# Two chained attention layers on one core: most second-layer blocks take their probabilities from transposed scores, normalised inside the exponential

## What is computed

```
layer 1:  theta, phi, g = W x + b (three 1x1 convolutions)
          y = softmax_m(theta^T phi) g ;  z = (1-w) x + w (Wz y + bz)
layer 2:  q, k (16 channels), v (128) = W z + b
          o = softmax_j(q^T k / 4) applied to v
          result = Wf [gamma*o ; z] + bf
```

## Time and profile before

| | |
|---|---|
| median of 3 runs | 532.09 us (531.92 to 532.65) |
| the profiled execution | 531.95 us, its span 529.9 |
| granted TensorE clock | 1.0 of full speed |
| PE, DVE, ACT, POOL busy | 97%, 76%, 68%, 49% of the span |
| moved by DMA | 15.24 MB, 29 GB/s on average |

### The profile page before, as it was taken

One profiled execution on the slowest core, in us unless ns is written; L12 is line 12 of the kernel. 1 busy time (PEld: TensorE's weight loads), 2 busy tenths in 40 slices (PEclk: granted clock), 3 DMA queues, 4 the chain that ended last, 5 costly groups with the idle time before them and its releaser, 6 DMA issues.

```text
span 529.9 us, 8447 instructions
## 1 busy us (share of the span) xinstructions
PE 516.4 (97%) x2933; PEld 437.1 (82%) x2933; DVE 404.7 (76%) x606; ACT 358.4 (68%) x652; POOL 257.3 (49%) x287
## 2 busy tenths in 40 slices
PE   7998999999999999999999999999999999899996
PEld 5777788888888888888888888888888888788886
DVE  5968676797677877788777887678768786888873
ACT  4865567567785677657776577765777557777763
POOL 1555246575175542864346751558426560354442
PEclk9999999999999999999999999999999999999999
DMA  5100000012000110002000020000200010001001
GB/s 191 45 5 2 7 9 0 2 41 67 9 21 0 67 42 9 21 0 100 17 1 21 1 103 13 1 22 24 83 9 20 2 42 27 9 0 36 13 30 40
DMA packets 6825, 15.24 MB, mean 29 GB/s; under 512 B 1280, under 2 KB 1792, under 8 KB 6784
## 3 DMA queue, kind: packets, MB, share of 16 engines
q1 hardware_dynamic: 6640, 14.57, 8.2%
q10 hardware_dynamic: 144, 0.13, 0.1%
HBM read 8.93 MB, written 4.19 MB: 25 GB/s over the span
## 4 chain that ended last, share of the span: by engine, by line
PE 92%; ACT 3%; DMA 2%; DVE 1%; issue 1%; POOL 0%; SPq 0%; ACTq 0%; DVEq 0%
PE trans L500 20%; PE accum L524 11%; PE accum L526 11%; PE accum L525 11%; PE scores L490 5%; PE scores L466 5%; PE scores L464 5%; PE scores L465 5%; PE misc L551 4%; PE misc L464 3%; PE misc L465 3%; PE misc L466 3%; PE misc L552 1%; DMA x_keep<-x_dram 1%; PE misc L556 1%; ACT probs L636 1%
## 5 line engine op out<-in xcount | busy, mean ns | idle before, releaser
L767 DVE TENSOR_TENSOR pt_lo<-trans,pt_hi 128x512 fp32r<-128x512 f32 x256 | 164.7, 685 | 65.6 <-ACT pt_hi L645 64.4
L645 ACT ACTIVATE pt_hi<-trans 128x512 fp32r<-128x512 f32 x256 | 138.8, 596 | 69.5 <-PE trans L500 67.8
L757 DVE TENSOR_REDUCE neg_max<-scores 128x1 f32<-128x1024 f32 x128 | 155.4, 1214 | 1.1 <-PE scores L466 1.1
L636 ACT ACTIVATE probs<-scores,neg_max 128x1024 f32<-128x1024 f32 x128 | 143.9, 1124 | 4.6 <-DVE neg_max L757 4.6
L500 PE MATMUL trans<-ident,probs 128*128 128x128 f32 x1024 | 133.7, 274 | 2.8 <-ACT probs L636 2.8
L500 PEld LDWEIGHTS trans<-ident,probs 128*128 128x128 f32 x1024 | 115.7, 141 | 14.4 <-ACT probs L636 4.6
L524 PE MATMUL accum<-pt_hi,g_hi 128*128 128x512 f32 x136 | 54.5, 401 | 0.0
L526 PE MATMUL accum<-pt_hi,g_lo 128*128 128x512 f32 x136 | 53.5, 393 | 0.0
L525 PE MATMUL accum<-pt_lo,g_hi 128*128 128x512 f32 x136 | 53.4, 392 | 0.0
L464 PE MATMUL scores<-phi_hi,theta_hi 128*128 128x512 f32 x112 | 48.8, 436 | 0.0
L490 PE MATMUL scores<-k_op,qk_op 128*128 128x512 f32 x128 | 45.4, 435 | 0.0
(11 more groups left out here) (144 smaller groups left out, 947.4 us busy)
## 6 DMA issues: line engine op xcount, KB each, us to landing
x_keep<-x_dram SPq DMA_DIRECT2D x8, 512.0 KB, 3.3
out_dram<-o_sb SPq DMA_DIRECT2D x15, 256.0 KB, 2.4
x_raw<-x_tiles_dram SPq DMA_DIRECT2D x7, 512.0 KB, 3.6
k_op<-qk_op SPq DMA_DIRECT2D x16, 96.0 KB, 2.3
x_raw<-x_tiles_dram SPq DMA_DIRECT2D x2, 256.0 KB, 3.6
...
```

Source lines behind the costliest of these rows:

```text
L636: nc.scalar.activation(probs[:, k % 2, :], scores[:, k % 2, :], ACT.Exp, bias=neg_max[:, k % 4:k % 4 + 1], accum_out=row_sum[:, slot(gb), ...
L645: nc.scalar.activation(pt_hi[:, gb % 2, 4 * bank:4 * bank + 4, t * P:(t + 1) * P], trans[:, cols(bank)].rearrange("p (n q) -> p n q", n=4) ...
L757: nc.vector.tensor_reduce(neg_max[:, k % 4:k % 4 + 1], scores[:, k % 2, :], AX.X, ALU.max, negate=True).then_inc(max_ready, 1)
L767: nc.vector.tensor_tensor(pt_lo[at], trans[:, cols(bank)].rearrange("p (n q) -> p n q", n=4), f(pt_hi[at]), ALU.subtract).then_inc(pt_lo_r ...
```

## The change

Eleven of the sixteen layer-2 blocks (`LATE`: those of index up to 24, the last being set aside as `ASIDE`) are made in another way; the last five, and all of layer 1, keep theirs ("turned").

For a late block PE still makes the scores with queries on the partitions, DVE the maximum, and ACT the exponential, but only for its row sum: the result overwrites the scores. Per pair of units ACT takes the logarithm of the sums; POOL forms `shift` = -max - log(sum) and splits it; SP writes it to a small DRAM tensor `turned` and reads it back along the columns, into two rows of `qk_op` that face ones in `k_op`. Later, nine steps after the block's start, PE multiplies again with the operands exchanged (keys on the partitions, queries along the columns), which gives score minus maximum minus log of the sum, transposed. One exponential of 128x1024 by ACT gives normalised probabilities; POOL rounds them to `pt_hi`, DVE subtracts for `pt_lo`. The value chunks of a late block begin at step 14 after its start instead of 6. No "r" group, diagonals and scaling are left for it: DVE adds the result to the other half and SP stores.

Other edits: `probs` becomes a ring of three tiles `fulls`; `neg_max` has 16 columns; diagonals and `r_rows` lie in tiles that are free by then; g and v of odd images take the tiles `g_hi_0`; the reciprocal waits for the reader of the old one; `k_op` gets two more memsets; ACT loads a function table with exponential and logarithm at the start.

```diff
+LATE = [gb for gb in range(len(BLOCKS)) if BLOCKS[gb][0] == 1 and gb <= 24]
+LATE_STEPS = {gb: tuple(TPB * gb + 9 + j for j in range(CPB)) for gb in LATE}
+LATE_STEPS[24] = (110, 111, 112, 113)
-HURRIED = {0: (6, 6, 7, 7), 1: (10, 10, 11, 11), 30: (126, 126, 127, 127), 31: (128, 128, 130, 131)}
+HURRIED = {0: (6, 6, 7, 7), 1: (10, 10, 11, 11), 24: (114, 114, 115, 115), 27: (116, 116, 117, 117), 30: (126, 126, 127, 127), 31: (128, 128, 130, 131)}
...
+                for gb in LATE:
+                    _, b, h = BLOCKS[gb]
+                    rows = turned[b, h]
+                    for pair in range(2):
+                        if k == TPB * gb + 3 + 2 * pair:
+                            sp.wait_ge(shift_split, 3 * pairs(gb, pair))
+                            sp.dma_start(rows[pair].rearrange("r t p -> p (r t)"), shift_parts[:, h, pair, :, :].rearrange("p r t -> p (r t)"),
+                                         allow_slow_non_contiguous=True).then_inc(shift_out[pair], 16)
+                    if k == TPB * gb + 7:
+                        for pair in range(2):
+                            sp.wait_ge(shift_out[pair], 16 * (LATE.index(gb) + 1))
+                        sp.dma_start(f(qk_op[b % 2][3 * CK:3 * CK + 2, cols(h)]).rearrange("r (q c) -> r q c", q=2),
+                                     rows.rearrange("q r t p -> r q (t p)")).then_inc(shift_in[h], 16)
...
+            def late_scores(gb, j):
+                _, b, h = BLOCKS[gb]
+                pe.wait_ge(shift_in[h], 16 * (b + 1))
+                for bank in range(2):
+                    trans_free(("late", gb, j), bank)
+                    tile = slice((2 * j + bank) * P, (2 * j + bank + 1) * P)
+                    last = nc.tensor.matmul(trans[:, cols(bank)], k_op[b % 2][:, tile], qk_op[b % 2][:, cols(h)],
+                                            start=True, stop=True)
+                last.then_inc(late_scores_ready, 1)
...
+            def pair_log(gb, pair):
+                at = slice(2 * pair, 2 * pair + 2)
+                act.wait_ge(probs_ready, units(TPB * gb + 2 * pair + 1))
...
+                nc.scalar.activation(log_sum[:, BLOCKS[gb][2], at], row_sum[:, slot(gb), at], ACT.Ln).then_inc(log_ready, 1)
...
+            def late_exp(gb, j):
+                act.wait_ge(late_scores_ready, late(gb, j))
+                full_free(act, ("late", gb, j))
+                nc.scalar.activation(full_of(("late", gb, j)), trans[:, :], ACT.Exp).then_inc(late_ready, 1)
...
+            def late_lo(gb, j):
+                dve.wait_ge(late_hi_ready, late(gb, j))
+                pair_free(dve, gb, j)
+                hi, lo = pair_tiles(gb, j)
+                nc.vector.tensor_tensor(lo, full_of(("late", gb, j)), f(hi), ALU.subtract).then_inc(late_lo_ready, 1)
...
+                for gb, j in late_fills(k - 2):
+                    late_lo(gb, j)
+                if 0 <= k - 2 < UNITS and (k - 2) // TPB in TURNED:
+                    unit_lo(k - 2)
...
+            def late_hi(gb, j):
+                pool.wait_ge(late_ready, late(gb, j))
+                pair_free(pool, gb, j)
+                hi, _ = pair_tiles(gb, j)
+                nc.gpsimd.tensor_copy(hi, full_of(("late", gb, j))).then_inc(late_hi_ready, 1)
```

538 lines of the change are left out of this document (325 added, 213 removed).

## The result

The changed kernel takes 534.22 us (median of 9 runs, 534.05 to 537.69) against 532.09 us for the kernel before (9 runs beside it, 531.92 to 534.07): ratio 1.0053, 95% interval 1.0033 to 1.0074. It is 0.5% slower where the forecast was 520.3 us, and it lies outside the range of 511 to 530. The profiled execution took 534.12 us, with a span of 532.3 us.

What follows compares the result with a forecast made beforehand. PE's own instruction stream was taken as the bound (busy 516.4 of 529.9 us). 529.9 - 23.1 + 3.5 + 3.0 + 3.9 + 0 + 1.0 = 518.2 us of span, 520.3 us with 2.05 beyond the span; range 511 to 530.

Steps and rivals of the forecast that it cites:

- What goes from PE: Eleven late blocks: transposes removed, two score matmuls per unit added, 18.0 us; row-scale matmuls removed, 5.1; 23.1 us shed.
- The tail: Steps 114 to 117, with twice the value chunks, and set-aside block's late work beside normal units: 0 us, bounds -2 and +4.
- The ramp: Steps 22 to 25 have no value chunks, so waits they covered appear on PE: 3.9 us, bounds 2 and 5.
- The repeats: Waits returning in the 16-step repeats: 3.5 us at projection drains by ACT, 3.0 us from DVE and POOL meeting.
- about 60.5 us instead of 63.0: Sign expected in the new profile: the length of one repeat of 16 steps after and before the change.
- The phi to v hand-over: ACT drains two PE groups in one step and comes later: 0.7 us wait per repeat, 3.5 in five, bounds 1.5 and 5.
- DVE and POOL: Late subtraction reading two SBUF tiles and POOL operations exclude each other: 0.6 us per repeat, 3.0 in all, bounds 0 and 12.
- Setup: Two more memsets at step 6 add 2.1 us on DVE, half reaching PE: 1.0 us, bounds 0 to 2.
- Rival 3: Shift's DRAM write and read exceed the 12 us available, so PE waits 11 times: 542 us at 14 us, chance 0.06.
- if PE waits for the DMA at the late scores: Sign at the second score matmuls that the forecast is wrong because the shift's transfers arrive late.
- Rival 2: DVE and POOL exclude each other on the path, 12 us instead of 3, tail +4: 533 us (526 to 533), chance 0.20.

Runs made afterwards that it cites:

- c1_no_fills: Changed kernel without block 24's late scores, exponential, cast and subtraction in steps 110 to 113: 527.01 us, ratio 0.9924 to the kernel before.
- c2_no_split: Changed kernel without POOL's cast and DVE's subtraction for block 24, its late scores and exponentials kept: 534.46 us, ratio 1.0051.
- e1_split_exp: Changed kernel with block 24's late exponential taken bank by bank, two instructions of 512 columns: 532.09 us, ratio 1.0003.
- c6_log: Changed kernel with ACT's logarithm behind the step's small drains instead of ahead of them: 533.49 us, ratio 1.0027.
- c3_reduce: Changed kernel with every late two-input DVE subtraction replaced by a one-input maximum over the same columns: 534.63 us (532.49 to 539.76), ratio 1.0058.
- c5_drain: Changed kernel with DVE draining a late block's accum ahead of the previous step's maximum in steps 42, 58, 74, 90: 535.56 us, ratio 1.0064.
- c4_setup: Changed kernel with the four k_op memsets moved from step 6 to DVE's start and step 5: 535.6 us, ratio 1.0076.
- c9_best: Changed kernel with k_op memsets moved, accum drained early, logarithm later, shift written in rows and gathered on reading, block 24's exponential halved: 525.80 us, ratio 0.9887.
- d1_rows: Changed kernel with the shift written as 128 pieces of 16 bytes instead of 512 of 4, landing in wrong places: 532.89 us, ratio 1.0025.

## Why the prediction was wrong

The forecast span was 518.2 us, the measured one 532.3: 14.1 us too little. By its own steps:

- **What goes from PE.** Right in kind: 672 transposes, 40 + 4 late exponentials and 10 r matmuls are left. The 23.1 us of work shed are borne out by these counts; what failed is what came back.
- **The tail, "I take 0 (bounds -2 and +4)".** This is the step that failed. Waits there cost 8.2 us: steps 108 to 117 grew by 15.6, of which 4 x 1.39 us are the moved value chunks and 4 x 0.46 the late scores. 6.0 of the 8.2 are the turns in `trans` (c1_no_fills, c2_no_split, e1_split_exp), and 2.2 lie in steps 114 to 117, where PE's rows name 0.99 us for `o_sb` and 0.78 for a small group (1.16 and 0.94 by starts); those I did not test. The offset that the prediction set against its waits did not come either: it took PE's 1.3 us wait for the exponential near the end to go, and that wait stands in step 109 in both kernels (1.34 before, 1.35 after). The prediction added up what each engine has to do in a step of 4.3 us and found it level. It did not ask how often the one bank pair is handed over in a step. The rows for it were there: it had worked out for one step of the ramp that `trans` comes free only after ACT's 0.8 and DVE's 1.2. With the late scores the loop of step 110, from one unit's scores to the next, is 2.28 us of PE's other work (440.12 to 442.40), 0.75 to the start of the exponential, 1.02 for it, 0.15 to PE's transposes and 0.82 for these: 5.02 us, the length of the step. For 1.2 of it PE's row is empty, since the next thing in its list needs the bank.
- **The ramp, 3.9 (bounds 2 and 5).** Mis-sized: steps 16 to 27 shed 10.7 us of work and became 4.7 shorter, so 6.0 came back. PE's rows name 4.4 of it: two waits of 0.97 for `values_full`, as forecast, 0.53 and 0.72 for the exponential and for `trans` (forecast 0.6 and 1.4), but also 0.49, 0.48 and 0.27 in steps 18 to 20, which the prediction took as covered. Counted by starts, as in step 110, these seven waits are 5.8 of the 6.0. No experiment was made on the ramp, so this is read from the trace alone.

```profile
86.53 0.50 PE L517 MATMUL misc<-x_hi,w_parts 128*128 128x512 f32 x1 [0.49 <-DVE values_full L902]
...
105.11 0.65 PE L631 MATMUL misc<-ident,ut 128*128 128x128 f32 x4 [0.97 <-DVE values_full L902]
109.41 0.39 PE L626 MATMUL misc<-w_parts,x_hi 128*128 128x256 f32 x1 [0.97 <-DVE values_full L902]
112.81 1.09 PE L560 MATMUL trans<-ident,fulls 128*128 128x128 f32 x8 [0.53 <-ACT fulls L721]
115.09 1.01 PE L570 MATMUL trans<-qk_op,k_op 128*128 128x512 f32 x2 [0.72 <-DVE pt_lo L871]
```

- **The repeats, 3.5 + 3.0.** 9.6 us came back in steps 28 to 107 where these two terms have 6.5. By the sum a repeat should be 2.9 us shorter, and it is 2.3 to 2.4. (The prediction's own sign, "about 60.5 us instead of 63.0", does not follow from its sum: 58.8 + 0.7 + 0.6 is 60.1. It took the 63.00 of a window for the repeat, which is 63.40.) Of the 9.6 the next two points name 7.4 (3.2, 1.7 and 2.5), step 33 is 1.4, and 0.8 is left.
- **The phi to v hand-over, 0.7 per repeat.** Right: steps 34, 50, 66, 82 and 98 should be 0.41 us shorter by the work shed, and they are 0.22 to 0.23 longer: 0.64 us came back, 3.2 in five. A third is the logarithm (c6_log).
- **DVE and POOL, 3.0 (bounds 0 and 12).** The mechanism is right, the size was 1.7 (c3_reduce). Beside it stood a wait that was not seen: `accum` of a late block behind a maximum, 0.6 us four times, 2.5 in all (c5_drain). Together they are 4.2, above the term. POOL's load is the plainest sign: the prediction has near 275 us, the changed kernel 307.8, and without the two-input subtraction it is 273.5.
- **Setup, 1.0 (0 to 2).** 1.3; the cause is right (c4_setup).
- **Rival 3, the shift's round trip.** The bound from a small transfer, 3.2 us, was too low: the write takes 8.5, since it goes in pieces of 4 bytes, and where POOL splits x the second write is issued at 131.4, the read behind it can be issued only at 142.5, and it lands at 145.8: 14.4 us where the prediction had 12 to spare. PE waits once in the profiled execution (step 33, 1.1 us by the row, 1.4 by c9_best's step), and 2.0 to 2.2 us at that step in those of c3_reduce, c4_setup and c5_drain. That is one of the prediction's own signs of being wrong ("if PE waits for the DMA at the late scores"). The prediction cited the Trainium skill ("DMA: Bandwidth & Descriptors", Rules for kernel authors), that such a pattern becomes one descriptor per element. That weighed the right way (8.5 us with pieces of 4 bytes, 1.9 with 16 in d1_rows), and the prediction gave it no term. It was not the 22 us of the rival. It may be behind the runs of the changed kernel above 534.4, but no such run was profiled, and in two of the three the clock was lower too (0.997).
- **Rival 2, 533 us.** The measured time lies near it, and that is chance: it was to come from 12 us of DVE and POOL excluding each other and from DVE's load in the tail. The first is worth 1.7 us (c3_reduce), the second nothing in steps 110 to 113 (c2_no_split).

So the forecast failed by the term of 0 for the tail (8.2 us: a missing chain through `trans`, 6.0, and 2.2 behind it), and by smaller errors of one sign: 3.1 in steps 28 to 107 (1.4 of it at step 33), 2.1 in the ramp, 0.3 in the setup, 0.3 behind the tail; together 14.0 of the 14.1.
